# Graph transformer and graph attention layers: the first stage's output projection as split products

## The chip, the cores and the metric
The kernel runs on one core of a Trainium2 chip. The metric is device microseconds of one execution. Engines are TensorE (PE; its weight loads are PEld), VectorE (DVE), ScalarE (ACT), GpSimd (POOL) and SyncE (SP), which issues the loads and stores. TensorE, VectorE, ScalarE and GpSimd each work through their instructions in the order in which the program has them and wait for one another through semaphores.

## The reference
64 graphs of 128 nodes with 256 features pass through a transformer layer (8 heads of 32, and a feed-forward part), and then through two graph attention layers. Only the first attention is touched:

```python
normed = layernorm(hidden, g1, b1)
q, k, v = normed @ Wq + bq, normed @ Wk + bk, normed @ Wv + bv     # 8 heads of 32
logits = q @ k.T / sqrt(32) + (2 * adj - 1)
weights = softmax(logits) * (0.25 + 0.75 * adj)
weights = weights / max(weights.sum(-1), 1e-6)
attended = weights @ v                                             # 128 x 256 per graph
hidden = hidden + attended @ Wo + bo                               # this product changes
```

All of it is in float32.

## The kernel before
All 64 graphs' features stay in SBUF (x_all). Four stages follow one another, each over 16 chunks of four graphs: A (layer norm, attention, output projection), B (the feed-forward part), and the two graph attention layers. Only A and the setup before it change.

**Products.** Where a product has to be exact, most stages split both factors: hi is the value rounded to the type fp32r, lo the rest, and hi*hi + hi*lo + lo*hi is summed (three, wide, tall: L1222 to L1224, L1238 to L1240). The weights are split in the setup (whl). The output projection does without: a_out multiplies att_t by wo_sb in float32, two matmuls of 256 columns per graph, which stand in the trace as two passes each (four records of L1346 per graph).

**Stage A.** It is a software pipeline. Every engine has its own a_step(i, half, par), called for i = 0 to 16; each call has two pairs pp = 0 and 1 ("first" and "second" pair of an iteration). In a pair TensorE computes the logits of two graphs (a_logits, L1313, into banks 0 to 3 of BK) and does the transposes of the exponentials in four groups (a_turn, L1320); for the two graphs before, s-2 and s-1, it does the attention (a_av, L1332, into bank 4), turns the attended rows (a_attn_turn, L1339, into bank 4 again), and projects graphs s-3 and s-2 (a_out, L1346, bank 5). Between these stand the products of the next chunk: in the first pair the turn of the normalised rows (ln_turn, L1247), of the adjacency (adj_turn, L1301), and three of the four q and k products (a_proj, L1222 to L1224); in the second the fourth of them and v (a_vproj, L1238 to L1240).

**The helpers' work per pair.** ScalarE: exponentials of four groups (a_exps, L1004), evictions, and the copy of the turned attended rows to SBUF (a_att_copy, L1010), which frees bank 4 for the next attention. VectorE: the maxima of the logits in two halves (a_max, L462), norm of the attended rows (a_norm, L473 to L478), product of the turned exponentials with the adjacency factor (a_pt_out, L468, four a pair), the sum of projection and residual (a_resid, L484), statistics (L297, L302) and in the first pair the lo part of the normalised rows (ln_lo, L314).

**Waits around the change.** a_turn of a group waits for its exponentials, those for the maximum of their half, the maximum for the logits. adj_turn and the first a_proj wait for ln_lo. a_attn_turn(s) waits for a_norm(s); a_av(s) for a_att_copy(s-1), as both results lie in bank 4; a_out(s) for a_att_copy(s). a_logits of a pair waits for all four a_pt_out of the pair before.

**Order.** The order on each engine is written out by hand in its a_step. On TensorE a first pair is: logits, ln_turn, av(s-2), out(s-3), adj_turn, turn 0, proj 0, attn_turn(s-2), turn 1, av(s-1), out(s-2), proj 1, turns 2 and 3, attn_turn(s-1), proj 2. A second pair is: logits, av(s-2), out(s-3), proj 3, turn 0, attn_turn(s-2), vproj 0, turn 1, av(s-1), out(s-2), vproj 1 and 2, turns 2 and 3, attn_turn(s-1), vproj 3. Iteration 1 has no out(s-3) in its second pair. After iteration 16 a short drain handles the last graphs. Iteration 0 computes no attention; in it VectorE runs setup_rows (L367 and after) and GpSimd and ScalarE prepare the weights of the later stages.

## Time and profile before
| | us |
|---|---|
| median of 3 runs | 1175.31 (1175.23 to 1177.13) |
| profiled execution | 1174.76 |
| its span, first to last instruction | 1173.0 |
| PE busy, of the span | 1089.1 (93%) |
| DVE busy | 782.1 (67%) |
| ACT busy | 742.5 (63%) |
| POOL busy | 426.4 (36%) |

Stage A lies between about 48 and 434 us, from the first logits (L1313) at 48.03 to the first product of stage B at 434.29. Matmuls overlap, and their ends are modelled, so it is the distance from start to start that tells what one costs. "x8" in a row of the timeline means that eight instructions of one kind are merged. Idle time in brackets stands with the engine and line that ended it.

### The profile page before, as it was taken

The numbers are of one execution on the slowest core, as the hardware profiler recorded it, in microseconds if no ns is written. First come the engines' busy times: TensorE is split into PE (matmuls) and PEld (weight loads), VectorE is DVE, ScalarE is ACT, GpSimd is POOL, SyncE is SP. The second block draws the span as 40 slices with busy tenths as digits, with TensorE's granted clock in tenths as the row PEclk, the third lists the DMA queues.
The fourth block names the chain that finished last, engine by engine and source line by source line (L and its number), as shares of the span: only waits on it lengthen the run. The fifth ranks groups of instructions, "written<-read, shape, count | busy, mean of one in ns | idle before, by whom it ended". The sixth has DMA issues, their size and how long they took to land.

```text
span 1173.0 us, 41366 instructions
## 1 busy us (share of the span) xinstructions
PE 1089.1 (93%) x16156; PEld 959.7 (82%) x16156; DVE 782.1 (67%) x1908; ACT 742.5 (63%) x1766; POOL 426.4 (36%) x641
## 2 busy tenths in 40 slices
PE   5699999999999989999999999997888888779998
PEld 5588888888888868998998899896777777678886
DVE  5677777767777765445545544554777777758886
ACT  2467776777767755435535544554777777568896
POOL 2541211212121203212311321213677766766764
PEclk9799999999999999999999999998999999979999
DMA  8021111111100000000000000000000000001212
GB/s 230 4 75 29 29 41 44 30 29 29 56 12 11 11 3 1 1 1 0 0 0 0 0 0 0 0 1 19 22 18 18 18 18 19 4 19 55 72 57 87
DMA packets 41737, 31.18 MB, mean 27 GB/s; under 512 B 5281, under 2 KB 41377, under 8 KB 41633
## 3 DMA queue, kind: packets, MB, share of 16 engines
q1 hardware_dynamic: 36736, 28.84, 7.9%
q10 hardware_dynamic: 4896, 0.80, 0.5%
q8 instruction: 83, 1.36, 0.5%
q14 instruction: 22, 0.17, 0.0%
HBM read 21.25 MB, written 8.39 MB: 25 GB/s over the span
## 4 chain that ended last, share of the span: by engine, by line
PE 74%; DVE 8%; issue 7%; ACT 6%; POOL 4%; ACTq 1%; DVEq 1%; DMA 0%; POOLq 0%
PE BK L1346 6%; PE BK L1224 5%; PE BK L1223 5%; PE BK L1222 5%; PE BK L1432 5%; PE BK L1430 5%; PE BK L1431 5%; PE BK L1320 4%; PE BK L1332 4%; PE F L1222 3%; PE BK L1313 3%; PE F L1247 3%; PE F L1224 3%; PE F L1223 3%; PE F L1238 2%
## 5 line engine op out<-in xcount | busy, mean ns | idle before, releaser
L1085 ACT ACTIVATE gf<-BK,bcol 128x512 f32<-128x512 f32 x128 | 88.3, 690 | 177.8 <-PE BK L1224 167.4
L876 POOL TENSOR_TENSOR ve<-mv,eps_l 128x4 f32<-128x4 f32 x64 | 15.3, 240 | 442.7 <-DVE mv L302 441.2
L1004 ACT ACTIVATE e_sb<-BK,nmx 128x128 f32<-128x128 f32 x512 | 141.8, 403 | 28.5 <-DVE nmx L462 28.5
L1430 PE MATMUL BK<-wf_hi,gh 128*128 128x256 f32 x512 | 142.8, 279 | 0.0
L1431 PE MATMUL BK<-wf_hi,gl 128*128 128x256 f32 x512 | 141.4, 276 | 0.0
L1432 PE MATMUL BK<-wf_lo,gh 128*128 128x256 f32 x512 | 141.4, 276 | 0.0
L555 DVE TENSOR_TENSOR gl<-gf,gh 128x512 fp32r<-128x512 f32 x128 | 93.8, 732 | 64.1 <-ACT gh L1086 62.2
L468 DVE TENSOR_TENSOR pt_sb<-BK,ft 128x512 f32<-128x512 f32 x128 | 85.3, 687 | 68.0 <-PE BK L1320 66.4
L1024 ACT ACTIVATE xn<-x_all,neg_mr,rstd 128x256 f32 (+1 forms) x188 | 99.9, 602 | 30.7 <-POOL neg_mr L885 15.7
L569 DVE TENSOR_TENSOR x_all<-BK,x_all 128x256 f32 (+1 forms) x64 | 27.2, 425 | 116.5 <-PE BK L1432 116.5
L1224 PE MATMUL BK<-xh,wf_lo 128*128 128x512 f32 x256 | 100.8, 394 | 0.0
L1223 PE MATMUL BK<-xl,wf_hi 128*128 128x512 f32 x256 | 100.4, 392 | 0.0
L1222 PE MATMUL BK<-xh,wf_hi 128*128 128x512 f32 x256 | 99.5, 389 | 0.5 <-DVE x_all L484 0.5
L297 DVE BATCH_NORM_STATS2 st<-x_all 128x6 f32 (+1 forms) x256 | 95.1, 412 | 7.1 <-DMA x_all<-in_x_dram 7.1
L1431 PEld LDWEIGHTS BK<-wf_hi,gl 128*128 128x128 f32 x512 | 96.2, 188 | 0.0
L1430 PEld LDWEIGHTS BK<-wf_hi,gh 128*128 128x128 f32 x512 | 96.1, 188 | 0.0
L1432 PEld LDWEIGHTS BK<-wf_lo,gh 128*128 128x128 f32 x512 | 96.1, 188 | 0.0
L853 POOL TENSOR_TENSOR x_all<-x_all,c_bc 128x256 f32 (+1 forms) x128 | 90.2, 738 | 5.8 <-POOL rp L929 5.1
L462 DVE TENSOR_REDUCE nmx<-BK 128x8 f32<-128x1024 f32 x64 | 76.7, 1220 | 23.0 <-PE BK L1313 23.0
L625 DVE SCALAR_TENSOR_TENSOR pp<-BK,gt_all 128x512 f32<-128x512 f32 x128 | 82.0, 684 | 14.1 <-PE BK L1476 10.3
L853 POOL TENSOR_TENSOR x_all<-x_all,bo_bc 128x256 f32 (+1 forms) x64 | 44.8, 732 | 124.1 <-ACT xn L1024 124.1
L1086 ACT ACTIVATE gh<-BK,bcol 128x512 fp32r<-128x512 f32 x128 | 87.1, 681 | 0.0
(216 smaller groups left out, 2988.6 us busy)
## 6 DMA issues: line engine op xcount, KB each, us to landing
x_all<-in_x_dram SPq DMA_DIRECT2D x16, 512.0 KB, 4.4
adj_in<-in_adj_dram SPq DMA_DIRECT2D x32, 256.0 KB, 2.8
out_dram<-y SPq DMA_DIRECT2D x16, 512.0 KB, 2.9
s_wf<-in_L_gnn_Wf_dram SPq DMA_DIRECT2D x2, 1024.0 KB, 11.4
s_w<-in_L_gnn_W_dram SPq DMA_DIRECT2D x2, 256.0 KB, 8.0
s_wq<-in_L_gnn_Wq_dram SPq DMA_DIRECT2D x1, 256.0 KB, 3.6
s_wk<-in_L_gnn_Wk_dram SPq DMA_DIRECT2D x1, 256.0 KB, 4.1
s_wv<-in_L_gnn_Wv_dram SPq DMA_DIRECT2D x1, 256.0 KB, 4.8
```

Source lines behind the costliest of these rows:

```text
L297: dve.bn_stats(st[:, g, :], xs(i, g)).then_inc(ln_st, 1)
L555: dve.tensor_tensor(gl[:, f, :], gf[f % 2][:], gh[:, f, :].bitcast(F32), ALU.subtract).then_inc(b_gl, 1)
L853: pool.tensor_tensor(xs(i, g), xs(i, g), bias[:], ALU.add).then_inc(signal, 1)
L1004: e = act.activation(e_sb[:, j, :], LE[:, r, q, :], ACT.Exp, bias=nmx[:, j:j + 1], scale=1.0)
L1024: act.activation(xn[:, g, :], xs(nxt, g), ACT.Identity, scale=rstd[:, g:g + 1], bias=neg_mr[:, g:g + 1]).then_inc(ln_xn, 1)
L1085: act.activation(gf[f % 2][:], BK[:, f % 4, :], ACT.Gelu, bias=bcol[:, 6 + f:7 + f])
L1222: pe.matmul(dst, w_hi, m_hi, start=start, stop=False)
L1223: pe.matmul(dst, w_hi, m_lo, start=False, stop=False)
L1224: return pe.matmul(dst, w_lo, m_hi, start=False, stop=stop)
L1430: pe.matmul(dst, gh[:, f, n], hi[:, f, :], start=(f == 0), stop=False)
L1431: pe.matmul(dst, gl[:, f, n], hi[:, f, :], start=False, stop=False)
L1432: r = pe.matmul(dst, gh[:, f, n], lo[:, f, :], start=False, stop=(f == FT - 1))
```

## The change
The weight wo is split like the others (whl["wo"]); its float32 copy moves from a buffer of its own to the space in which the other weights are staged, and VectorE splits it at the start of setup_rows. b_wide, used in the setup alone, now lies in e_sb. att_t gives way to three tiles: att_f (float32), att_h and att_l (fp32r).

ScalarE copies the turned rows to att_f, and later (a_att_hi) rounds att_f to att_h. VectorE (a_att_lo) subtracts att_h from att_f and writes att_l. a_out waits for a_att_lo and does six matmuls of 256 columns in place of two in float32. The projections, the low part and the sum take other places in a pair.

```diff
             def setup_rows():
 
+                split("wo", None)
                 for n, b in enumerate((bv_col[:], cols[:, 22:24], cols[:, 26:28])):
...
+            def a_att_lo(s):
+                dve.wait_ge(a_ah, s + 1)
+                wait_for(dve, a_wo, s)
+                dve.tensor_tensor(att_l[:], att_f[:], att_h[:].bitcast(F32), ALU.subtract).then_inc(a_al, 1)
...
                     if not first:
                         a_max(sp, 1)
+                    if old:
+                        a_att_lo(s - 3)
                     if back:
                         a_norm(s - 2)
-                    if old:
-                        a_resid(*((i - 2, 1) if pp == 0 else (i - 2, 3)), s - 3)
                     if not first:
                         a_pt_out(sp, 1 - par, pp, 0)
...
                     if not first:
                         a_pt_out(sp, 1 - par, pp, 1)
+                    if old:
+                        a_resid(*((i - 2, 1) if pp == 0 else (i - 2, 3)), s - 3)
...
                     if not first:
                         a_pt_out(sp, 1 - par, pp, 2)
+                    if back:
+                        a_att_lo(s - 2)
+                    if not first:
                         a_pt_out(sp, 1 - par, pp, 3)
...
             a_step(NC, NC // 2, 0)
+            a_att_lo(NG - 3)
             a_norm(NG - 2)
             a_resid(NC - 1, 1, NG - 3)
+            a_att_lo(NG - 2)
             a_norm(NG - 1)
             a_resid(NC - 1, 2, NG - 2)
+            a_att_lo(NG - 1)
             a_resid(NC - 1, 3, NG - 1)
...
             def a_att_copy(s):
                 act.wait_ge(a_at, s + 1)
+                wait_for(act, a_al, s)
+                act.activation(att_f[:], AT_ps, ACT.Copy).then_inc(a_ac, 1)
+
+            def a_att_hi(s):
+                act.wait_ge(a_ac, s + 1)
                 wait_for(act, a_wo, s)
-                act.activation(att_t[:], AT_ps, ACT.Copy).then_inc(a_ac, 1)
+                act.activation(att_h[:], att_f[:], ACT.Copy).then_inc(a_ah, 1)
...
                     back = not (isinstance(s, int) and s < 2)
+                    if not (isinstance(s, int) and s < 3):
+                        a_att_hi(s - 3)
                     if pp == 0:
                         ln_hi(i + CA)
...
                     if not first:
                         a_exps(sp, 2)
                         a_exps(sp, 3)
+                    if back:
+                        a_att_hi(s - 2)
...
             def a_out(s):
-                pe.wait_ge(a_ac, s + 1)
+                pe.wait_ge(a_al, s + 1)
                 wait_for(pe, a_x, s)
+                hi, lo = whl["wo"]
                 for kt in range(KT):
-                    m = pe.matmul(WO_ps, att_t[:, kt * P:(kt + 1) * P], wo_sb[:, kt, :], start=(kt == 0), stop=(kt == KT - 1))
+                    n = slice(kt * P, (kt + 1) * P)
+                    pe.matmul(WO_ps, att_h[:, n], hi[:, kt, :], start=(kt == 0), stop=False)
+                    pe.matmul(WO_ps, att_l[:, n], hi[:, kt, :], start=False, stop=False)
+                    m = pe.matmul(WO_ps, att_h[:, n], lo[:, kt, :], start=False, stop=(kt == KT - 1))
                 m.then_inc(a_wo, 1)
...
                     if back:
                         a_av(s - 2, sp - 1, *before, 0)
-                    if old:
-                        a_out(s - 3)
...
                     if pp == 0 and not tail:
                         a_proj(i, 0)
+                    if old:
+                        a_out(s - 3)
                     if back:
                         a_attn_turn(s - 2)
...
                     if back:
                         a_av(s - 1, sp - 1, *before, 1)
-                        a_out(s - 2)
...
                         else:
                             a_vproj(i, 3)
+                    if back:
+                        a_out(s - 2)
```

## Rows read from the trace of the kernel before

**Rows 1.** Windows: PE, PEld, DVE, ACT, POOL busy, PE clock, DMA share, GB/s
```profile
76.00:409.00 333.00, 328.77 (x6030) 285.31 (x6029) 244.89 (x544) 239.80 (x709) 59.70 (x109) 1.00 0.11 31
409.00:434.30 25.30, 20.09 (x497) 15.33 (x496) 18.25 (x39) 13.26 (x42) 2.20 (x4) 1.00 0.02 4
```

**Rows 2.** Timeline of TensorE, a first pair: start, duration, engine, line
```profile
240.12 1.17 PE L1313 MATMUL BK<-k,q 32*128 32x128 f32 x32
...
243.01 1.13 PE L1346 MATMUL BK<-wo_sb,att_t 128*128 128x256 f32 x4
243.98 0.60 PE L1301 MATMUL F<-ident,adj_in 128*128 128x128 f32 x4
244.41 0.60 PE L1320 MATMUL BK<-ident,e_sb 128*128 128x128 f32 x4
...
246.23 0.38 PE L1339 MATMUL BK<-ident,att 128*128 128x128 f32 x2
...
247.26 0.83 PE L1332 MATMUL BK<-v,pt_sb 128*32 128x33 f32 x64 [0.21 <-ACT att_t L1010]
...
250.37 1.04 PE L1320 MATMUL BK<-ident,e_sb 128*128 128x128 f32 x8
251.24 0.38 PE L1339 MATMUL BK<-ident,att 128*128 128x128 f32 x2
...
252.93 0.83 PE L1313 MATMUL BK<-k,q 32*128 32x128 f32 x19
```

**Rows 3.** Timeline of TensorE, the second pair just before
```profile
228.92 1.17 PE L1313 MATMUL BK<-k,q 32*128 32x128 f32 x32
...
233.08 0.60 PE L1320 MATMUL BK<-ident,e_sb 128*128 128x128 f32 x4
...
238.04 1.04 PE L1320 MATMUL BK<-ident,e_sb 128*128 128x128 f32 x8
```

**Rows 4.** Timeline of TensorE, the second pair of iteration 1
```profile
61.02 1.17 PE L1313 MATMUL BK<-k,q 32*128 32x128 f32 x32
62.12 0.77 PE L1332 MATMUL BK<-v,pt_sb 128*32 128x33 f32 x64
62.82 0.50 PE L1222 MATMUL F<-xh,wk_hi 128*128 128x512 f32 x1
63.16 0.40 PE L1223 MATMUL F<-xl,wk_hi 128*128 128x512 f32 x1
...
64.72 0.66 PE L1320 MATMUL BK<-ident,e_sb 128*128 128x128 f32 x4 [0.23 <-ACT e_sb L1004]
```

**Rows 5.** Timeline of TensorE, first and last of eleven v products
```profile
236.75 0.28 PE L1239 MATMUL F<-wv_hi,xl 128*128 128x256 f32 x1
...
237.92 0.28 PE L1240 MATMUL F<-wv_lo,xh 128*128 128x256 f32 x1
```

**Rows 6.** Timeline of ScalarE in the first pair of rows 2
```profile
242.96 1.15 ACT L1004 ACTIVATE e_sb<-BK,nmx 128x128 f32<-128x128 f32 x4
...
246.73 0.38 ACT L1010 ACTIVATE att_t<-BK 128x256 f32<-128x256 f32 x1 [0.39 <-PE BK L1339]
```

**Rows 7.** Timeline of VectorE at the end of the second pair
```profile
238.68 1.29 DVE L468 TENSOR_TENSOR pt_sb<-BK,ft 128x512 f32<-128x512 f32 x2 [2.05 <-PE BK L1320]
```

**Rows 8.** Timeline of TensorE, the last output projection
```profile
432.64 1.13 PE L1346 MATMUL BK<-wo_sb,att_t 128*128 128x256 f32 x4 [0.47 <-ACT att_t L1010]
```

**Rows 9.** Groups of the first 60 us: line, form, count, busy, mean ns
```profile
L973 ACT ACTIVATE w_hi<-w_g 128x512 fp32r<-128x512 f32 x2 | 1.1, 630 | 0.0
L436 DVE TENSOR_TENSOR wst_lo<-wst,wst_hi 128x256 fp32r<-128x256 f32 x2 | 0.8, 425 | 0.1
```

**Rows 10.** Timelines of VectorE and GpSimd in the setup
```profile
25.66 0.69 DVE L408 TENSOR_TENSOR prod<-s_w,a_bc 128x512 f32<-128x512 f32 x1 [0.56 <-DVE msc L401]
...
27.11 3.63 DVE L408 TENSOR_TENSOR prod<-s_w,a_bc 128x512 f32<-128x512 f32 x1
...
26.59 3.60 POOL L862 TENSOR_TENSOR wf_g<-s_wf,cols 128x2048 f32<-128x2048 f32 x1 [14.21 <-DMA s_wf<-in_L_gnn_Wf_dram]
```

More of the change, by code:

```diff
@@ L85, in build @@
         for name, kt, n in (("wq", KT, D), ("wk", KT, D), ("wv", KT, D), ("wf1", KT, FF),
-                            ("wf2", FT, D), ("w1", KT, D), ("w2", KT, D), ("wst1", KT, P), ("wst2", KT, P)):
+                            ("wf2", FT, D), ("w1", KT, D), ("w2", KT, D), ("wo", KT, D), ("wst1", KT, P), ("wst2", KT, P)):
             if name == "wf1":
@@ L89, in build @@
             whl[name] = [sb(f"{name}_{part}", [P, kt, n], F32R) for part in ("hi", "lo")]
-        wo_sb = sb("wo_sb", [P, KT, D])
         bo_bc, bf2_bc, c1_bc, c2_bc = (sb(n, [P, D]) for n in ("bo_bc", "bf2_bc", "c1_bc", "c2_bc"))
@@ L137, in build @@
         stage = {"wq": o("s_wq", [P, KT, D]), "wk": o("s_wk", [P, KT, D]), "wv": o("s_wv", [P, KT, D]),
-                 "wo": wo_sb, "wf1": o("s_wf1", [P, KT, FF]), "wf2": o("s_wf2", [P, FT, D]),
+                 "wo": o("s_wo", [P, KT, D]), "wf1": o("s_wf1", [P, KT, FF]), "wf2": o("s_wf2", [P, FT, D]),
                  "w1": o("s_w1", [P, KT, D]), "w2": o("s_w2", [P, KT, D])}
@@ L159, in build @@
         att = o("att", [P, D])
-        att_t = o("att_t", [P, D])
+        att_f = o("att_f", [P, D])
+        att_h = o("att_h", [P, D], F32R)
+        att_l = o("att_l", [P, D], F32R)
         nmx = o("nmx", [P, 2 * H])
@@ L163, in build @@
         rinv = o("rinv", [P, H])
-        b_wide = [o(f"b_wide{n}", [P, KT, P]) for n in range(3)]
+        b_wide = [e_sb[:, 2 * n:2 * n + 2, :] for n in range(3)]
         o = overlay(base_of_region, base_of_region + REGION)
@@ L236, in build @@
         a_et, a_ft, a_qk, a_qkev, a_v, a_vev = (sem(n) for n in ("a_et", "a_ft", "a_qk", "a_qkev", "a_v", "a_vev"))
-        a_l, a_nm, a_e, a_tt, a_pt, a_o, a_rs, a_ri, a_att, a_at, a_ac, a_wo, a_x = (
-            sem(n) for n in ("a_l", "a_nm", "a_e", "a_tt", "a_pt", "a_o", "a_rs", "a_ri", "a_att", "a_at", "a_ac",
+        a_l, a_nm, a_e, a_tt, a_pt, a_o, a_rs, a_ri, a_att, a_at, a_ac, a_ah, a_al, a_wo, a_x = (
+            sem(n) for n in ("a_l", "a_nm", "a_e", "a_tt", "a_pt", "a_o", "a_rs", "a_ri", "a_att", "a_at", "a_ac", "a_ah", "a_al",
                              "a_wo", "a_x"))
@@ L368, in setup_rows @@
             def setup_rows():
+                split("wo", None)
                 for n, b in enumerate((bv_col[:], cols[:, 22:24], cols[:, 26:28])):
-                    done(dve.tensor_copy(b_wide[n][:], b.unsqueeze(2).to_broadcast([P, KT, P])))
+                    done(dve.tensor_copy(b_wide[n], b.unsqueeze(2).to_broadcast([P, KT, P])))
                 dve.wait_ge(s_ident, 6)
@@ L1073, in _ @@
             a_step(NC, NC // 2, 0)
+            a_att_hi(NG - 3)
             a_att_copy(NG - 2)
+            a_att_hi(NG - 2)
             a_att_copy(NG - 1)
+            a_att_hi(NG - 1)
             def b_step(i, half, par):
```

## The prediction
> **What bounds the kernel now.** The granted clock and the busy time by stage come first. From 76 to 409 us, where the attention stage runs in its steady pattern, TensorE's clock is 1.00 (the 2.4 GHz level) and its matmuls are busy 328.77 of 333 us, VectorE 244.89, ScalarE 239.80 [rows 1]. That looks like a stage in which every microsecond taken from TensorE comes off the time. TensorE's timeline says how far that is true. One iteration (four graphs, two pairs) takes 240.12 - 228.92 = 11.20 us for the second pair, which comes first in these rows, and 252.93 - 240.12 = 12.81 for the first pair of the next iteration [rows 2, 3]: 24.0 us. In it the reader is to see the four output projections (L1346), and that after the logits (L1313) other work stands before the first transposes of the exponentials (L1320), which need logits, maximum and exponentials to be through. That latency is what the change runs into.
>
> The Trainium skill, "Perfetto Trace Analysis", section "Identifying the Most-Contended Engine", says that matmul busy time is a poor measure and that LDWEIGHTS' share should be read. Here that is 285.31/333 = 0.86 against 0.99 [rows 1]. By the matmul row TensorE has 1% to spare, by the other one cannot say that it is full; the starts below decide.
>
> **1. The product itself.** Before, a projection is four passes of 256 columns. The first of a pair's starts at 243.01, the next work at 243.98: 0.97 us [rows 2]. Some of this is not the product's but the price of turning from the 32-column attention tiles to a full array: in the second iteration, which has no projection in this place, attention starts at 62.12, L1222 at 62.82, L1223 at 63.16; the 0.34 of that first L1222 against 0.23 for later ones of the kind (0.23 x 6 = 1.38, the 1.82 from 244.41 to 246.23 less 0.44 for four transposes, half of the 0.87 that eight take between 250.37 and 251.24) leaves 0.11 [rows 2, 4]. It stays, in front of whatever follows attention. So 0.86 us are the product's. After, it is six 256-column passes of the split kind; eleven starts of such passes from 236.75 to 237.92 are 0.117 apart [rows 5], so 0.70. Gain 0.16 us a graph. Taken at the bound, 64 x 0.16 = 10.4 us.
>
> **2. First pair of an iteration, front half.** The projection of graph s-3 leaves the place between attention and the adjacency turn, so the transposes of group 0 could start 0.86 sooner than 244.41. They can't: ScalarE's four exponentials of group 0 start at 242.96 and end at 244.11 [rows 6]. How long TensorE takes after a ScalarE end is seen at att_t: 246.73 + 0.38 = 247.11, attention starts at 247.26, so 0.15 [rows 2, 6]. Nothing before these exponentials is changed: they wait for logits, layer norm turn and both xh evictions. The new ScalarE copy att_h that is put ahead of them fits into the time up to 241.99, which the layer norm turn sets. Hence 244.26, only 0.15 sooner, of the 0.86. Then 1.82 for transposes and L1222 to L1224, then the projection moved here, 0.70, and only then the turn of the attended rows (L1339), 0.70 - 0.15 = 0.55 later than its 246.23. The second attention (247.26) waits for the copy of that turn, 0.55 later too. The new subtraction att_l on VectorE stands behind the second maximum and delays the norm of s-2 by 0.33, but the turn needs it only 0.55 later: covered.
>
> **3. First pair, back half.** From 247.26 on, 0.86 goes (the projection ahead of L1222), 0.70 comes at the pair's end: -0.16. Its own chain is att_h behind the exponentials of groups 2 and 3, att_l behind the third pt_sb, and 1.38 of projection lies beside it. Sum of the pair: +0.39 us.
>
> **4. Second pair.** Here the trace holds the new order already. In iteration 1 logits start at 61.02, attention, then L1222 to L1224 with no output projection between; the transposes of group 0 start at 64.72, after 0.23 us idle on the exponentials: 3.70 us [rows 4]. In the steady pair it is 233.08 - 228.92 = 4.16 [rows 3]. So 0.46 sooner, then 0.70 for the moved projection: the turn of s-2 is 0.24 later, about what its norm on VectorE needs, since att_l ahead of it takes 0.33. Then the projection before L1238 goes, -0.86, and one comes at the end, +0.70. That makes +0.08. But the present pair ends with a wait: 250.37 to 251.24 gives 0.87 for the eight transposes, the turn 0.22, six passes 0.70 and some 0.10 to enter the logits, 1.89 from 238.04, so TensorE was ready at 239.93 and the logits started at 240.12, when the last two pt_sb on VectorE (238.68 + 1.29, + 0.15) were done [rows 2, 3, 7]. After, TensorE needs 2.59 behind the transposes' start, VectorE 0.64 to its start + 1.29 + 0.33 for att_l between the two + 0.15 = 2.41: TensorE is last and the 0.19 wait goes. Sum of the pair: -0.11.
>
> An iteration thus costs +0.28 us (0.39 - 0.11); 14 steady iterations (2 to 15) +3.9. Its bounds: if the releases take 0.08 less than I read and every att_l is fully hidden, +0.1; if att_l or att_h comes some tenths late at the end of a second pair, +0.55. So +1.4 to +7.7.
>
> **5. The drain after 409 us.** There TensorE is busy 20.09 of 25.30 us [rows 1]: latency counts. The last projection waits 0.47 for att_t and starts at 432.64 [rows 8]. Two steps come into that chain: att_h (a 512-column copy from SBUF takes 0.63 and a 256-column one from PSUM 0.38; I take 0.41) and att_l (0.43 for this form), with two releases of 0.05 and 0.10 more [rows 6, 9]. That is +0.99, less 0.26 for the shorter product and its shorter last pass: +0.75. The two pairs before it each have att_l ahead of a norm for which TensorE already waits, some 0.35, and nearly the same saved at the projection: +0.2 each. In all +1.2, bounds 0.3 and 2.5.
>
> **6. Setup.** Splitting wo adds two copies and two subtractions to VectorE in iteration 0, from rows of the same shape 2 x 0.2 + 2 x 0.36 + two waits, 1.3 us with the pipelining (0.43 is one subtraction's full length, rows 9). VectorE's row sets this stretch. 0.56 of it falls into the idle time before the first prod at 25.66 [rows 10]. The second prod lasted 3.63 us against 0.69, and ended 0.5 us behind GpSimd's wf_g (26.59 + 3.60) [rows 10]. With prod starting near 26.35, it is still ahead of wf_g, and much of the remaining 0.7 is swallowed where the second prod stands still anyway; if prod comes behind 26.59, it stands still itself and its successor with it. I take +0.5, bounds 0 and 2.5.
>
> The page "SBUF — State Buffer" of the Trainium skill, section "Who interferes with whom", says that a VectorE operation with two SBUF inputs and a GpSimd one that reads SBUF exclude each other, and the first to start keeps the port. The 3.63 us agree. By it a prod that starts first would hold wf_g back by up to 0.5, which is the +0.5; one that starts second costs 1.5 to 2.4. It speaks against the change, and is in the upper bound.
>
> The other added instructions, att_h (64 x 0.41) and att_l (64 x 0.43), add 26 and 28 us to engines that are idle 93 and 88 us of the steady stretch [rows 1]; they cost only in the places named. b_wide in e_sb's space is read before the first exponential, no cost. No DMA is added.
>
> **Sum.** 3.9 + 1.2 + 0.5 = +5.6 us on the profiled execution's 1174.76, so 1180.4. The profiled execution lies 0.55 below the median 1175.31, within the runs' spread, so I add nothing for it: 1180.4.
>
> **Rivals.**
> A, TensorE's own work decides (faster). The trace shows 0.99 busy, and the second pair gains already. Mechanism: the exponentials come sooner than the old positions say, because the layer norm turn or the maxima had been held back by the pattern, so the transposes' wait doesn't eat the 0.86. It decides if the transposes of group 0 in the first pair start under 3.7 us after the logits. Then 64 x 0.16 = 10.4 off, 1.7 back: 1166. Against it: the one pair that has the new order waits for these exponentials already, 0.23 us idle [rows 4].
> B, a draw (within 0.2%, about the smallest difference this kernel's measurement can tell): iterations cost +0.1 or less and setup hides: 1.4 + 0.3 to 1.2 gives 1177.
> C, att_l is late in each second pair. It stands ahead of the last pt_sb, and if att_h behind eight exponentials comes after the third pt_sb, pt_sb and the next logits are held: 0.5 to 0.8 us per iteration on top: 1190.
> D, the simple count from start to start, 0.97 against 0.70, 64 x 0.27 = 17 off and nothing back, 1158: it forgets the 0.11 that stay.
>
> **How the numbers follow.** Forecast 0.54, B 0.20, A 0.16, C 0.08, D 0.02. The likeliest one's own range is 1177.5 to 1185.5, from the bounds. Stretched into A until 2 in 10 are outside: 1170 to 1187. Faster by over 0.2% 0.20 (A, D and a little of B's spread), within 0.2% 0.22, slower 0.58.
>
> **What would show it.** After the change: ten or more of the first pairs with logits to group 0 at 4.1 us and an idle or stretched time before the adjacency turn or these transposes, released by VectorE's xl and ScalarE's e_sb; second pairs at 3.70; a pair of 13.2 and one of 11.1; L1339 in the first pair 6.65 us behind the logits instead of 6.11. An iteration under 23.7 us would prove the forecast wrong and A right; one over 24.7 would prove C. A drain of more than 27.5 us, or VectorE's setup ending over 1 us later, would make terms 5 or 6 wrong.

## The result, and the profile after
The changed kernel takes 1180.77 us, the median of 8 runs (1177.83 to 1185.95), against 1175.24 (8 runs, 1173.59 to 1178.23) for the kernel before: a ratio of 1.0049, 95% interval 1.003 to 1.0068. It is slower by more than 0.2%, and 0.4 us above the forecast of 1180.4. The profiled execution took 1179.88 us, its span is 1178.1, 5.1 more than before.

That a total fits says little, so the span is first cut into segments, at starts read from TensorE's timeline: the first row of the logits of each pair (L1313 before, L1340 after), and the first product of stage B. Stages B to D are counted up to the start of the last matmul, 4.6 us before the end of the span in every profile. Both kernels were profiled three times (e8 to e11 are the second and third profiles). All numbers are us; the last two columns are the median length of a first and of a second pair in iterations 2 to 15. The experiments stand here too, since all are read by this table.

| kernel | to the start of iteration 2 | iterations 2 to 15 | last pair and drain | stages B to D | first pair | second pair |
|---|---|---|---|---|---|---|
| before | 72.13 | 335.55 | 26.60 | 734.09 | 12.77 | 11.20 |
| before (e9) | 72.87 | 335.26 | 26.56 | 733.47 | 12.77 | 11.16 |
| before (e11) | 72.80 | 334.93 | 26.55 | 734.49 | 12.77 | 11.16 |
| after | 72.95 | 337.18 | 28.01 | 735.32 | 12.95 | 11.14 |
| after (e8) | 73.17 | 337.17 | 30.86 | 735.32 | 12.95 | 11.14 |
| after (e10) | 72.97 | 337.17 | 29.13 | 734.21 | 12.95 | 11.13 |
| e1, order alone | 72.63 | 347.95 | 27.20 | 736.80 | 13.37 | 11.44 |
| e2, product alone | 72.72 | 326.78 | 26.49 | 733.19 | 12.44 | 10.88 |
| e3, new order in float32 | 73.16 | 346.16 | 30.24 | 732.51 | 13.27 | 11.45 |
| e4, projection in the gap | 73.13 | 333.50 | 28.12 | 733.97 | 12.76 | 11.07 |
| e5, filler | 74.86 | 337.99 | 28.01 | 738.14 | 12.95 | 11.18 |
| e6, gap, two buffers | 72.61 | 326.97 | 28.38 | 731.86 | 12.45 | 10.88 |
| e7, split later | 72.51 | 337.17 | 28.03 | 732.95 | 12.95 | 11.13 |
| e12, drain filled | 72.83 | 337.73 | 28.19 | 736.03 | 12.95 | 11.18 |

The pairs repeat to 0.04 us, the middle segments of one kernel to 0.6. Stages B to D, the same code in all, repeat to 1.1 within a kernel and lie between 731.86 and 738.14 over all of them. By the means of three profiles the change adds 0.4 us up to iteration 2, 1.9 in iterations 2 to 15, 2.8 in the last pair and the drain, and 0.9 in stages B to D: 6.0.

The windows of the steady stretch, after (columns as in [rows 1]):

```profile
76.00:409.00 333.00, 321.76 (x6104) 281.25 (x6105) 262.50 (x599) 255.54 (x762) 59.21 (x108) 1.00 0.11 31
```

Matmul busy time fell by 7 us against [rows 1] while the stretch became longer; VectorE and ScalarE rose by 18 and 16. TensorE's timeline of a first pair and the second one behind it (as [rows 2, 3]):

```profile
241.54 1.17 PE L1340 MATMUL BK<-k,q 32*128 32x128 f32 x32
...
243.67 0.76 PE L1359 MATMUL BK<-v,pt_sb 128*32 128x33 f32 x64
244.81 0.63 PE L1328 MATMUL F<-ident,adj_in 128*128 128x128 f32 x4 [0.37 <-DVE xl L315]
245.51 0.66 PE L1347 MATMUL BK<-ident,e_sb 128*128 128x128 f32 x4
...
247.40 0.28 PE L1375 MATMUL BK<-wo_hi,att_h 128*128 128x256 f32 x1
247.52 0.28 PE L1376 MATMUL BK<-wo_hi,att_l 128*128 128x256 f32 x1
...
248.10 0.38 PE L1366 MATMUL BK<-ident,att 128*128 128x128 f32 x2
...
249.05 0.76 PE L1359 MATMUL BK<-v,pt_sb 128*32 128x33 f32 x64
...
254.49 1.17 PE L1340 MATMUL BK<-k,q 32*128 32x128 f32 x32
...
258.19 0.66 PE L1347 MATMUL BK<-ident,e_sb 128*128 128x128 f32 x4 [0.24 <-ACT e_sb L1019]
...
259.38 0.38 PE L1366 MATMUL BK<-ident,att 128*128 128x128 f32 x2
```

In the place that the projection left, between attention and the adjacency turn, TensorE now stands still for 0.37 us until VectorE's xl is there; then the four adjacency transposes take 0.70 from start to start instead of 0.43 [rows 2], since the next ones have to wait for the exponentials. Those of group 0 start 3.97 us behind the logits (before: 4.29). In the second pair they start at exactly 3.70, with the same idle time of a quarter microsecond that iteration 1 showed before [rows 4]. ScalarE's side of it:

```profile
244.31 1.15 ACT L1019 ACTIVATE e_sb<-BK,nmx 128x128 f32<-128x128 f32 x4
...
248.52 0.38 ACT L1025 ACTIVATE att_f<-BK 128x256 f32<-128x256 f32 x1 [1.32 <-PE BK L1366]
```

The exponentials end at 245.46, the transposes start at 245.51. The waits of the steady stretch say that this is so every time: engine, line, what it waited for, us in total, times, longest.

```profile
PEld BK L1347 <- ACT e_sb L1019: 13.7, 28, 0.7
...
PE F L1328 <- DVE xl L315: 5.2, 14, 0.4
PE BK L1347 <- ACT e_sb L1019: 3.3, 14, 0.2
```

The end of the drain, as [rows 8], with the two new steps ahead of the last projection (timelines of ScalarE, VectorE and TensorE):

```profile
435.32 0.38 ACT L1025 ACTIVATE att_f<-BK 128x256 f32<-128x256 f32 x1 [1.88 <-PE BK L1366]
435.74 0.42 ACT L1030 ACTIVATE att_h<-att_f 128x256 fp32r<-128x256 f32 x1
436.18 0.43 DVE L486 TENSOR_TENSOR att_l<-att_f,att_h 128x256 fp32r<-128x256 f32 x1 [0.81 <-ACT att_h L1030]
436.66 0.39 PE L1375 MATMUL BK<-wo_hi,att_h 128*128 128x256 f32 x1 [1.38 <-DVE att_l L486]
```

And the setup, as [rows 10] (timelines of VectorE, GpSimd and ScalarE):

```profile
22.08 0.48 DVE L332 CAST wo_hi<-s_wo 128x256 fp32r<-128x256 f32 x2
22.60 0.76 DVE L338 TENSOR_TENSOR wo_lo<-s_wo,wo_hi 128x256 fp32r<-128x256 f32 x2
...
26.48 0.69 DVE L410 TENSOR_TENSOR prod<-s_w,a_bc 128x512 f32<-128x512 f32 x1
26.93 3.70 POOL L877 TENSOR_TENSOR wf_g<-s_wf,cols 128x2048 f32<-128x2048 f32 x1 [14.47 <-DMA s_wf<-in_L_gnn_Wf_dram]
...
27.93 3.25 DVE L410 TENSOR_TENSOR prod<-s_w,a_bc 128x512 f32<-128x512 f32 x1
...
43.43 1.09 ACT L1044 ACTIVATE xn<-x_all,neg_mr,rstd 128x256 f32<-128x256 f32 x2 [14.38 <-POOL neg_mr L900]
```

The first prod starts 0.82 later than in the profile before; the first xn, which waits for what follows it, 0.45 later (it was 42.98).

### The profile page after: what moved, and what is told of

Its sections match the earlier page's. It is cut to its first block, busy times and chain, and to the rows that moved or that the text cites. A ratio compares the mean times of both kernels' runs of the same rounds, so it can differ in the third digit from the quotient of the medians.

```text
span 1178.1 us, 41904 instructions
## 1 busy us (share of the span) xinstructions
PE 1082.6 (92%) x16284; PEld 957.3 (81%) x16284; DVE 803.3 (68%) x1976; ACT 762.6 (65%) x1830; POOL 427.1 (36%) x641
## 4 chain that ended last, share of the span: by engine, by line
PE 67%; DVE 9%; ACT 8%; issue 7%; POOL 6%; ACTq 1%; DVEq 1%; DMA 0%; POOLq 0%
PE BK L1251 5%; PE BK L1250 5%; PE BK L1249 5%; PE BK L1464 5%; PE BK L1463 5%; PE BK L1462 5%; PE BK L1347 5%; ACT e_sb L1019 3%; PE BK L1340 3%; PE F L1249 3%; PE F L1265 2%; PE F L1274 2%; PE F L1251 2%; PE F L1250 2%; DVE nmx L464 2%
## 5 line engine op out<-in xcount | busy, mean ns | idle before, releaser
L470 DVE TENSOR_TENSOR pt_sb<-BK,ft 128x512 f32<-128x512 f32 x128 | 88.0, 687 | 45.0 <-PE BK L1347 45.0
```

## The experiments
The theory was the prediction's: the split product saves 0.16 us a projection, the new order takes more than that back, because it empties the place in which TensorE's work covered the wait for the exponentials. The rivals: TensorE's work alone decides; or the cost is the added helpers', att_h and att_l.

**The two halves of the change, each alone.** e1 keeps the float32 product and att_t (two of them, which the new order needs) and takes only the order.

```diff
-                    if old:
-                        a_out(s - 3)
                     if pp == 0:
                         adj_turn(i)
...
                         a_proj(i, 0)
+                    if old:
+                        a_out(s - 3, 1)
                     if back:
                         a_attn_turn(s - 2)
```

> The kernel before with the new order alone: float32 product (0.86 us), no att_h and att_l, two att_t tiles so that the copy needn't wait for the projection two places later; b_wide in e_sb, no split of wo. Theory (the moved projection no longer fills the time in which the first transposes wait for their exponentials): group 0's transposes start 3.97 and 3.70 us after the logits as in the changed kernel, and each pair is longer than in it by 2 x 0.16: 13.27 and 11.46, an iteration 24.7, so 14 x 0.75 = +10.5: 1185.5 us. Rival (the loss comes from the added work on ScalarE and VectorE and its waits): without them the order costs nothing, 1175 to 1177.

Measured: 1188.41 us (4 runs, 1186.78 to 1191.0), ratio 1.0115 [1.01, 1.0129]. Pairs of 13.37 and 11.44 us. The order alone costs 12.7 us in iterations 2 to 15 (347.95 less the mean of the three profiles before, 335.25), and this kernel has no helper that could be blamed. The total is 2.9 us above what was expected. 2.2 us of that lie in iterations 2 to 15, for which +10.5 was expected. In this profile stages B to D, which the edit doesn't touch, are 2.8 longer than before as well, but the profiled execution, 1191.0, is also the slowest of the four.

e2 keeps the order and takes the product. The low parts are left out: six fp32r passes with the same rounded operands, so only the shape of the work is that of the change.

```diff
-        att_t = o("att_t", [P, D])
+        att_t = o("att_t", [P, D], F32R)
...
-                    m = pe.matmul(WO_ps, att_t[:, kt * P:(kt + 1) * P], wo_sb[:, kt, :], start=(kt == 0), stop=(kt == KT - 1))
+                    for n in range(3):
+                        m = pe.matmul(WO_ps, att_t[:, kt * P:(kt + 1) * P], wo_r[:, kt, :], start=(kt == 0 and n == 0), stop=(kt == KT - 1 and n == 2))
```

> The kernel before with six fp32r passes in the old places, att_t written as fp32r, wo rounded; the low parts of both factors are left out, the six passes all use the high parts. Theory: 0.16 us a graph comes off as long as the transposes stay behind their exponentials: the first pair from 12.77 to 12.45, the second from 11.20 to 10.9, 14 x 0.62 = 8.7 and some in the drain: 1166 us. Rival (the product isn't shorter in the pipeline, or VectorE's pt_sb sets the pairs): 1173 to 1176.

Measured: 1166.33 us (6 runs), ratio 0.9936 [0.9919, 0.9952]. Iterations 2 to 15 are 8.5 us shorter, 8.47 / 56 projections = 0.15 each, and group 0 keeps its cover:

```profile
262.23 0.97 PE L1349 MATMUL BK<-wo_r,att_t 128*128 128x256 f32 x6
263.05 0.60 PE L1303 MATMUL F<-ident,adj_in 128*128 128x128 f32 x4
263.48 0.60 PE L1322 MATMUL BK<-ident,e_sb 128*128 128x128 f32 x4
```

The row of six is 0.82 from start to start where the four float32 ones took 0.97 [rows 2].

**The helpers.** e3 is the changed kernel, with att_f, att_h, att_l and all waits, but its product is in float32 again, of att_h and wo_hi (the low parts are computed and left out of the product).

```diff
-                    pe.matmul(WO_ps, att_h[:, n], hi[:, kt, :], start=(kt == 0), stop=False)
-                    pe.matmul(WO_ps, att_l[:, n], hi[:, kt, :], start=False, stop=False)
-                    m = pe.matmul(WO_ps, att_h[:, n], lo[:, kt, :], start=False, stop=(kt == KT - 1))
+                    m = pe.matmul(WO_ps, att_h[:, n].bitcast(F32), hi[:, kt, :].bitcast(F32), start=(kt == 0), stop=(kt == KT - 1))
```

> The changed kernel with the float32 product of att_h and wo's high part in the same places and with the same waits; low parts left out of the product, though still computed. Theory: in the changed kernel every projection stands where TensorE is last, so the 0.16 us a graph is wholly visible: 64 x 0.16 = +10.4, 1191 us, iterations of 24.7. With the first experiment at the same iteration, att_h and att_l would cost nothing in steady state. Rival (helpers set the pace): under 1185, and more than the first experiment by several us at equal iterations.

Measured: 1188.93 us (4 runs), ratio 1.0128 [1.0113, 1.0142]. The pairs are 13.27 and 11.45 us, no longer than e1's without helpers: the 64 copies and 64 subtractions cost nothing in the steady pattern. e3 also closes the account. In iterations 2 to 15 the order costs 346.16 - 335.25 = +10.9, the product under that order brings 337.17 - 346.16 = -9.0, and under the old order -8.5 (e2). Per iteration that is 0.78 against 0.64. Why e1's first pair is 0.10 us longer than e3's, with less work around it, stays open, so the order's price is 10.9 to 12.7 us.

**Is TensorE full?** e5 is the changed kernel with more work in the two places where group 0 is waited for: two passes of 512 columns ahead of proj 3 in the second pair, two transposes ahead of the adjacency turn in the first. Their results aren't used.

```diff
+                if n == 3:
+                    for kt in range(KT):
+                        pe.matmul(F[0][:], whl["wk"][0][:, kt, P:2 * P], xh[:, kt, :], start=True, stop=True, skip_group_check=True)
...
+                if first == CA:
+                    for g in range(2):
+                        pe.transpose(F[0][:, g * P:(g + 1) * P], adj_in[par][:, g, :], ident[:])
```

> The changed kernel with TensorE work that nobody uses, put where the theory says that TensorE waits for the exponentials: two more passes of 512 columns ahead of the fourth q and k product (0.46 us, second pair) and two more transposes of the adjacency (0.22 us, first pair), 16 times each: 10.9 us of TensorE work. Theory: the transposes of group 0 stay at 3.70 to 3.75 and 3.97 us after the logits, an iteration stays at 24.1, the time within 1.5 us of the changed kernel: 1180 to 1182. Rival (TensorE's own work sets the pace everywhere): iterations of 24.8, 1190 to 1191.

Measured: 1185.35 us (5 runs, 1184.08 to 1187.14), ratio 1.0092 [1.0076, 1.0109]: between the two expectations, so the total decides nothing and the segments must. Group 0 starts at 247.79 - 243.82 = 3.97 us in the first pair, as without the filler, and at 260.54 - 256.78 = 3.76 in the second:

```profile
243.82 1.17 PE L1346 MATMUL BK<-k,q 32*128 32x128 f32 x32
...
247.09 0.41 PE L1332 MATMUL F<-ident,adj_in 128*128 128x128 f32 x2 [0.38 <-DVE xl L315]
247.34 0.60 PE L1334 MATMUL F<-ident,adj_in 128*128 128x128 f32 x4
247.79 0.66 PE L1353 MATMUL BK<-ident,e_sb 128*128 128x128 f32 x4
...
256.78 1.18 PE L1346 MATMUL BK<-k,q 32*128 32x128 f32 x32
...
258.58 0.73 PE L1314 MATMUL F<-xh,wk_hi 128*128 128x512 f32 x2
...
260.54 0.60 PE L1353 MATMUL BK<-ident,e_sb 128*128 128x128 f32 x4
```

The filler is two passes of 0.23 and two transposes of 0.11 per iteration, 0.68 x 14 = 9.5 us; iterations 2 to 15 took it in for 0.81. That refutes a TensorE that is full in these two places. Behind the wait it is full: e3's longer product costs its whole length there, 9.0 us for 56 projections. The rest of the 4.6 us over the changed kernel is elsewhere: 2.8 to 3.9 in stages B to D, which I can't explain (1.5 of it lies in one idle stretch of TensorE that ends at 862.44, for which the profile names no releaser), and 1.8 before iteration 2. The latter has a cause of its own, which the filler ran into by accident (timelines of VectorE and GpSimd):

```profile
26.29 3.60 POOL L877 TENSOR_TENSOR wf_g<-s_wf,cols 128x2048 f32<-128x2048 f32 x1 [13.55 <-DMA s_wf<-in_L_gnn_Wf_dram]
26.44 3.46 DVE L401 SCALAR_TENSOR_TENSOR scl<-grp 40x1 f32<-40x1 f32 x1
```

A one-column operation, which took 0.15 us in the changed kernel, stood still for 3.46 behind GpSimd's wf_g. VectorE came to it 0.4 us later than in the changed kernel (26.01), the transfer that wf_g waits for was there 0.6 sooner, and so wf_g was first. The first prod then starts at 31.03 instead of 26.48, and the first xn at 45.39 instead of 43.43.

**Filling the gap again.** If the lost cover is the cause, the projection of s-3 belongs back between attention and adjacency turn. e4 does that in the first pair, puts it behind proj 3 and ahead of group 0's transposes in the second, and moves att_l of s-3 ahead of the second maximum in both; the split of wo is as in the change.

```diff
                         a_max(sp, 0)
+                    if old:
+                        a_att_lo(s - 3)
...
+                    if pp == 0 and old:
+                        a_out(s - 3)
                     if pp == 0:
                         adj_turn(i)
```

> The changed kernel with the projection of s-3 put back into the time before the first transposes (first pair: between attention and the adjacency turn, second: behind the fourth projection of q and k), att_l of s-3 right behind the first maximum. Theory: first pair: transposes at about 4.06 to 4.2, then nothing but 1.82 us of products before the turn of the rows, so 12.95 - 0.70 + 0.15 = 12.4; second pair: 4.0 instead of 3.70, 11.14 - 0.70 + 0.3 = 10.75; iteration 23.15, 14 x 0.95 less than the changed kernel: 1167 us, faster than both. Rival (att_h and att_l late in their new place): no better than the changed kernel, 1180 or more, with a wait on att_l in front of the projection.

Measured: 1175.33 us (11 runs), ratio 1.001 [0.9998, 1.0023]. 5.4 us better than the change, and 8 short of what was expected. The first pair's rows name the reason (GpSimd, VectorE, TensorE):

```profile
240.91 2.99 POOL L868 TENSOR_TENSOR x_all<-x_all,bo_bc 128x256 f32 x4 [8.71 <-ACT xn L1044]
...
242.52 0.79 DVE L486 TENSOR_TENSOR att_l<-att_f,att_h 128x256 fp32r<-128x256 f32 x1
243.23 1.28 DVE L315 TENSOR_TENSOR xl<-F,xh 128x512 fp32r<-128x512 f32 x2
243.36 0.39 PE L1375 MATMUL BK<-wo_hi,att_h 128*128 128x256 f32 x1 [0.33 <-DVE att_l L486]
...
257.66 0.44 PE L1366 MATMUL BK<-ident,att 128*128 128x128 f32 x2 [0.15 <-DVE att L480]
```

att_l took 0.79 us instead of 0.42, in the very stretch in which GpSimd adds bo_bc to x_all; xl and the second maximum behind it are late by that much, and the projection waits 0.33 for it. That the overlap is the cause is shown by e4's other att_l: all 35 that no GpSimd operation overlaps took 0.41 to 0.43. In the second pair the norm is late in its turn. VectorE's path from maximum to exponentials has no room for a subtraction, so the order was right only in what it gave TensorE.

**Both conditions met.** e6 gives att_f, att_h and att_l two buffers each. The projection of s-4 then has its operands ready long before the gap, in both pairs, and no subtraction stands between the maxima. The split of wo moves to the end of the setup.

```diff
-        att_f = o("att_f", [P, D])
+        att_f = [o(f"att_f{r}", [P, D]) for r in range(2)]
...
+                    if far:
+                        a_out(s - 4, 0)
                     if pp == 0:
                         adj_turn(i)
...
-                    if old:
-                        a_out(s - 3)
...
+                    if old:
+                        a_out(s - 3, 1)
```

> The changed kernel with two tiles each of att_f, att_h and att_l, so that the projections can run later: that of s-4 stands in the gap before the first transposes in both pairs, that of s-3 between the v or q products and the third group of transposes; att_l never behind the first maximum nor ahead of a pt_sb; wo is split in setup_biases. Theory: first pair: transposes of group 0 at about 4.1, the turn of the rows at 5.9, the next logits at 12.3; second: 4.4 and 10.9; an iteration 23.2, 14 x 0.9 = 12.5 under the changed kernel: 1168 us. Rival (what limits is the chain through VectorE's norm and pt_sb, as in the projection in the gap): 1174 to 1176.

Measured: 1166.5 us (6 runs, 1165.52 to 1169.37), ratio 0.9937 [0.9921, 0.9952]: 0.6% faster than the kernel before and the best complete version here. Pairs of 12.45 and 10.88 us are e2's, with the full split product and all its helpers. Group 0 starts 4.14 us behind the logits, behind a projection instead of behind a wait.

```profile
259.38 1.17 PE L1341 MATMUL BK<-k,q 32*128 32x128 f32 x32
...
263.09 0.60 PE L1329 MATMUL F<-ident,adj_in 128*128 128x128 f32 x4
263.52 0.60 PE L1348 MATMUL BK<-ident,e_sb 128*128 128x128 f32 x4
```

**The split of wo in the setup.** e7 is the changed kernel with that split behind setup_biases, where VectorE waits for TensorE.

```diff
             def setup_rows():
-                split("wo", None)
...
+                split("wo", None)
```

> The changed kernel with wo split at the start of setup_biases, where VectorE waits 5 us for TensorE. Theory (the split held up VectorE's row in the setup by 0.45 us, and with it everything behind): ScalarE's first xn in iteration 0 back from 43.43 to 42.98 us, the logits of iteration 2 at about 72.4 instead of 72.95. Rival (the half microsecond comes from a later landing of the loads, GpSimd's wf_g started at 26.93 instead of 26.59): no difference.

Measured: one run, 1177.07 us, which alone can't be told from 1180.77. The split now lies in idle time (40.69 to 41.95, before the wait that ends at 45.71), and the 0.56 us idle ahead of the first prod is back:

```profile
25.86 0.69 DVE L409 TENSOR_TENSOR prod<-s_w,a_bc 128x512 f32<-128x512 f32 x1 [0.56 <-DVE msc L402]
...
43.08 1.09 ACT L1044 ACTIVATE xn<-x_all,neg_mr,rstd 128x256 f32<-128x256 f32 x2 [14.25 <-POOL neg_mr L900]
```

The first xn starts 0.35 earlier than in the changed kernel (0.45 expected), and iteration 2 starts at 72.51 against 72.95: -0.44. Against the three profiles of the changed kernel (mean 73.03) it is 0.5. By itself e7 doesn't decide, since its wf_g also started 0.60 sooner (26.33 against 26.93), which was the rival. The whole table does: the seven profiles without the split at the start of setup_rows reach iteration 2 at 72.13 to 72.87 (mean 72.61), six with it at 72.83 to 73.17 (mean 73.04), e5 set apart. So about 0.4 us of the start belongs to where the split stands.

**The same two kernels again.** e8 and e10 are the changed kernel, e9 and e11 the kernel before, without any edit. They were to show what of the segments is scatter.

> The changed kernel once more, for a second profile. If the differences in stages B to D between kernels (731.9 to 738.1 us in nine profiles) are scatter from run to run, that segment comes out a microsecond or more from 735.3, while pairs stay at 12.95 and 11.14 (within 0.03). If they were a cost of the change, it stays within 0.3 of 735.3. In the setup, wf_g's start (26.93 us, it waits for a transfer) should move by some tenths; if it comes ahead of VectorE's first prod (26.48), the first xn comes up to 2 us later than 43.43.

> The kernel before once more. Scatter: stages B to D a microsecond or more from 734.1, pairs at 12.77 and 11.20 (within 0.03), first prod at 25.66 ahead of wf_g in any case (idle 0.56 before it), first xn within 0.3 of 42.98.

> The changed kernel a third time, as the second: pairs 12.95 and 11.14, stages B to D off 735.3 by scatter, first xn at 43.4, or up to 2 us later if wf_g starts ahead of prod.

> The kernel before a third time: pairs 12.77 and 11.20, stages B to D off 734.1 by scatter, first xn within 0.3 of 42.98.

Measured, single times: 1182.93 and 1179.89 us changed, 1174.57 and 1175.18 before. The pairs came as expected. Stages B to D scattered less than I had thought: 735.32, 735.32 and 734.21 after, 734.09, 733.47 and 734.49 before, so the 0.9 between the means may be real in part. A part of the scatter is TensorE's granted clock. When the matmuls of stages B to D are divided into eight shares of equal number, the last eighth took 146.2 to 147.1 us in the five profiles with a mean clock of 0.96 or 0.97 in it (e2, e3, e4, e6, e7), and 147.7 to 149.2 in the nine with 0.94 or 0.95. In e8 wf_g started at 26.60, ahead of what was then the first prod (26.73, 4.02 us long instead of 0.69), but the first xn at 43.72 only, 0.3 later than in the first profile: the second prod no longer stood still, so most was made up.

What I had not looked for is in the last pair and the drain: 26.6 us in all three profiles before, but 28.01, 30.86 and 29.13 after. The windows tell why (e8, columns as in [rows 1]):

```profile
410.00:415.00 5.00, 3.89 (x112) 3.12 (x110) 3.84 (x5) 4.55 (x15) 2.80 (x4) 1.00 0.01 3
415.00:420.00 5.00, 4.38 (x80) 3.76 (x80) 3.33 (x11) 2.73 (x12) 0.00 (x0) 0.66 0.02 5
420.00:425.00 5.00, 3.64 (x108) 3.05 (x108) 3.83 (x7) 1.43 (x6) 0.00 (x0) 1.00 0.01 3
425.00:430.00 5.00, 4.10 (x78) 3.77 (x80) 2.96 (x7) 3.17 (x14) 0.00 (x0) 0.66 0.01 2
```

The granted clock, 1.00 before (2.4 GHz), averages 0.66 in two of these windows: for part of them it was at the lower level, 1.2 GHz. TensorE's timeline in e8 shows what that does, and what came before:

```profile
414.31 0.66 PE L1347 MATMUL BK<-ident,e_sb 128*128 128x128 f32 x4 [1.08 <-ACT e_sb L1019]
415.58 0.45 PE L1375 MATMUL BK<-wo_hi,att_h 128*128 128x256 f32 x1 [0.61 <-DVE att_l L486]
...
417.32 1.06 PE L1347 MATMUL BK<-ident,e_sb 128*128 128x128 f32 x4
```

Two waits of 1.08 and 0.61 us, then the same four transposes take 1.06 instead of 0.60. In e10 the window from 415 to 420 is at 0.66 too. In the first profile the drain was spared, and stage B paid at its start:

```profile
438.00:440.00 2.00, 1.85 (x4) 1.49 (x5) 0.09 (x1) 0.00 (x0) 0.00 (x0) 0.53 0.00 0
```

The three profiles before have 1.00 in every window from 400 us to 440. So the longer waits of the new drain cost their own length, 1.4 us, and in each profile a lower clock on top: 2.9 in e8, 1.1 in e10, and in the first profile about 1.3 at stage B's start (its first 1137 matmuls, an eighth, took 174.79 us against 173.26 to 173.87 before). Kernels made from the changed one spread alike. In e3 the clock was 0.68 from 425 to 430 (drain 30.24), in e7 it fell at the start of stage B (first eighth 175.31). In e5 the drain has the same waits (1.07, 0.61, 1.82 us) and the same length, 28.01, and every 5 us window from 400 to 465 is at 1.00 (TensorE's timeline of e5):

```profile
416.82 0.66 PE L1353 MATMUL BK<-ident,e_sb 128*128 128x128 f32 x4 [1.07 <-ACT e_sb L1019]
418.08 0.39 PE L1381 MATMUL BK<-wo_hi,att_h 128*128 128x256 f32 x1 [0.61 <-DVE att_l L486]
```

**The drain filled.** e12 is the changed kernel with 20 passes of 512 columns in the drain's waits (3, 1, 7, 1, 1, 2 and 5; the expectation counts 19), to keep TensorE at work; the results aren't used.

```diff
+            def keep_busy(n):
+                pe.wait_ge(ln_xl, CB * KT + 2)
+                for _ in range(n):
+                    pe.matmul(F[0][:], whl["wk"][0][:, 0, P:2 * P], xh[:, 0, :], start=True, stop=True, skip_group_check=True)
...
+                    else:
+                        keep_busy(3 if pp == 0 else 7)
...
             a_attn_turn(NG - 1)
+            keep_busy(5)
             a_out(NG - 1)
```

> The changed kernel with 19 more passes of 512 columns (0.23 us each, 4.4 us of work) in the drain's waits, results unused. Theory: in the drain of the changed kernel TensorE idles more than before, and its granted clock falls there in each of three profiles (to 0.66 in the 5 us windows), never in three of the kernel before; that costs 1 to 3 us in the drain and at the start of stage B. With the waits filled the clock stays at 1.00 until stage B is under way, last pair and drain take 28.0 to 28.5 us, the first eighth of stages B to D (1137 matmuls) 173.3, and the median falls by about 2 us, to 1178.5 to 1179. Rival: the clock falls for another reason; then it falls here too, or the work added costs some of its 4.4 us: 1181 to 1184.

Measured: 1180.44 us (6 runs, 1178.44 to 1181.17), ratio 1.0046 [1.0033, 1.0059]. The profile came out as the theory said, with 1.00 in all windows of the drain although there is more work in it:

```profile
415.00:420.00 5.00, 4.48 (x91) 3.52 (x90) 4.49 (x13) 3.26 (x12) 0.00 (x0) 1.00 0.02 5
```

Last pair and drain took 28.19 us (28.0 to 28.5 expected), the first eighth of stage B to D 173.88. The median did not follow: 1178.5 to 1179 was expected, and 1.0046 can't be told from 1.0049. That idling lets the clock fall is not shown by this one profile, since e5 has 1.00 with the same waits left empty.

What the clock means for the median can be read from the runs, each of which has its mean granted clock on record. Within a kernel the slow runs are those with a low clock: the changed kernel took 1177.83 us at 0.985 and 1182.95 and 1185.95 at 0.977. At 0.983 to 0.985 the two kernels still lie 6.0 us apart (medians 1179.88 of 3 runs and 1173.87 of 25), so most of the change's cost stands without a lower clock. And e12's six runs all have 0.983 to 0.985 and are no faster; whether the added passes or scatter took back what the clock gave isn't shown.

## Why the prediction was right, point by point
The forecast rests on three terms, and on nothing for stages B to D. Set beside the segments, in us (means of three profiles each, and for the drain the part that is there without a lower clock):

| term | predicted | measured |
|---|---|---|
| iterations 2 to 15 | +3.9 | +1.9 |
| drain | +1.2 | +1.4 |
| lower clock in the drain | not seen | +1.3 (0, 2.9, 1.1) |
| setup, with iteration 1 | +0.5 | +0.4 |
| stages B to D | 0 | +0.9 |
| sum | +5.6 | +6.0 (spans), medians +5.5 |

**Sign and mechanism were right.** The product saves 0.16 us a projection (step 1; e2 0.15, e3 0.16), and the new order takes back more, through the wait for the exponentials (steps 2 and 4; e1 and e3). e5 shows that TensorE has room where group 0 is waited for, against rival A, by which its own work decides. Matmul busy time was 0.99 of the steady stretch before [rows 1] and 321.76/333 = 0.97 after, and still 9.5 us of filler went into it for 0.8. The Trainium skill ("Perfetto Trace Analysis", "Identifying the Most-Contended Engine") calls this row a poor measure of how near its limit a kernel is; the trace agrees.

**The first pair was over-sized**, +0.39 predicted, +0.18 measured (12.77 to 12.95), and this is the term that was wrong. The prediction added to the one pair that it read, 12.81, and came to 13.20; from 12.95 that is 0.25 off, in three places:
- The turn (L1366) comes at 6.56 instead of 6.65: 0.09. Group 0 starts at 3.97, not 4.14. Its exponentials began 2.77 us behind the logits, not 2.84, and the transposes 0.05 behind the last exponential, not the 0.15 that I had taken from att_t. About half of that is lost again between there and the turn.
- From the turn to the second attention 0.95 us passed, not 1.03: 0.08. The copy att_f started 0.42 behind the turn, att_t had taken 0.50 [rows 2, 6].
- The back half took 5.44 us, not 5.52: 0.08.

I had added up pauses of the old pattern as if each were a fixed latency, though a part of each was slack.

**Second pair**: 3.70 was met to the hundredth, but the pair gained 0.02 to 0.06 instead of 0.11. The wait on pt_sb that it was to lose, 0.19, is in neither kernel's list of TensorE's waits, but it shows in the starts: from the last pass of a second pair to the next logits 0.38 us before (239.74 to 240.12) and 0.21 after (265.42 to 265.63). What is missing from the gain is mostly ahead of the turn: it starts 1.19 us behind group 0 (258.19 to 259.38), where 1.13 had been reckoned, 0.43 for the transposes and 0.70 for the projection.

**Rival C**, att_l late at the end of the second pair, did not happen: e1 and e3 have the same second pairs, with and without it.

**Drain**: the chain from the copy to the last projection is 436.66 - 435.32 = 1.34 us, before 432.64 - 432.20 = 0.44: +0.90 where the step had +0.99. 0.17 came off behind it, not 0.26. Net +0.73 for +0.75. What the step lacked is the clock: it counted idle time at its own length only, while a stretch that TensorE had got through at 1.00 fell to 0.66 in two of the three profiles.

**Setup**: prod came ahead of wf_g as reckoned, by 0.45 us, and the split costs about 0.4 at iteration 2. In the profile on which the term was read the path is another one than that sum, though: the second prod ends 0.55 us behind wf_g both before (30.74 and 30.19) and after (31.18 and 30.63), so the 0.45 of the first xn is wf_g's. 0.34 of it is the later landing of its transfer (26.93 for 26.59), which varies between profiles of one kernel too (26.59, 27.29 and 26.88 before), and 0.10 its greater length behind prod. That the size came out is partly luck. The feared case, 1.5 to 2.4 in the upper bound of this term, is real: in e5 the first xn came 1.96 later. The Trainium skill ("SBUF — State Buffer", "Who interferes with whom") has the rule: two SBUF inputs on VectorE and a GpSimd operation that reads SBUF exclude each other, and the first to start keeps the port for its whole length. The trace agrees for VectorE: prod 3.25 and 4.02 for 0.69, scl 3.46 for 0.15, att_l 0.79 for 0.42. The other way round it shows less: wf_g took 3.70 for 3.60 behind a prod that ran on 0.24 us into it.

**So the closeness of 1180.4 is partly luck.** The steady term was 2.0 too high, and a lower clock in the drain and 0.9 in stages B to D, neither of which I had, made up for it. Why stages B to D take 0.9 longer, and up to 6 us more in one kernel than in another, stays open but for the part of the clock told above. The first, third and last eighth of them vary (in e5 the fourth and seventh too, by 1.5 and 1.1 us), the second was 167.59 in every profile.

## What to carry to other kernels
In a pipeline whose engines wait for each other within a pair, the place of a piece of work counts more than its length: over iterations 2 to 15 the shorter product brought -8.5 us where the projections stayed in the time in which the first transposes wait for their exponentials, while with the projections moved behind it the total was +1.9, as the order cost 10.9 and the product brought -9.0. Before shortening work on the busiest engine, put some filler into its waits: if it vanishes, what is to be looked for is an order that covers the latency, and the buffers it needs (e6). And profile the same kernel more than once before a segment of a microsecond is called an effect: three profiles found the term that one had hidden.

## What the runs showed of the hardware
- A product of 256 rows of contraction by 256 columns takes 0.86 us in float32 (0.97 from start to start, less 0.11 for the turn from the 32-column tiles, which stays) and 0.70 as six fp32r passes (0.117 each): three products cost less than one.
- VectorE's smallest operations aren't safe from GpSimd: a 40x1 one took 3.46 us instead of 0.15 in e5, and whether VectorE or GpSimd came first changed between profiles of one kernel (26.93 behind 26.48, 26.60 ahead of 26.73).
- TensorE's granted clock fell from 1.00 (a mean of 0.66 over 5 us) behind waits of 1.08 and 0.61 us in two of three profiles of one kernel. In the third, where it fell later, at the start of stage B, and in e5, where it didn't fall, the same waits were followed by 1.00. At the lower clock four transposes took 1.06 us instead of 0.60.
